# A stage of a two-layer pair kernel: the z product contracts 64 partitions instead of 128, and its padding and the clearing of it go

## The reference, cut to what matters

```python
g = sigmoid(xn @ Wg + bg)                    # xn: group norm of x; 128 -> 128 channels
z = einsum('bikc,bkjc->bijc', a, b)          # 16 channels
x1 = x + g * (layer_norm(z, g2, b2) @ Wz + bz)   # z: 16 -> 128 channels
```

## Time and profile before

| | us |
|---|---|
| median of 3 runs | 4713.67 |
| the profiled execution, its own time | 4714.6 |
| its span, first to last instruction | 4712.9 |
| PE busy with matmuls | 3987.0 |
| DVE busy | 3935.2 |
| ACT busy | 3377.8 |
| POOL busy | 2670.3 |
| first to last z product of stage 4 | 1165.5 to 1937.7 |

### The profile page before, as it was taken

One profiled execution on the slowest core, in us unless ns is written; L12 is line 12 of the kernel. 1 busy time (PEld: TensorE's weight loads), 2 busy tenths in 40 slices (PEclk: granted clock), 3 DMA queues, 4 the chain that ended last, 5 costly groups with the idle time before them and its releaser, 6 DMA issues. The chain is left out here.

```text
span 4712.9 us, 89415 instructions
## 1 busy us (share of the span) xinstructions
PE 3987.0 (85%) x26438; PEld 2239.9 (48%) x26438; DVE 3935.2 (83%) x5450; ACT 3377.8 (72%) x4840; POOL 2670.3 (57%) x1428
## 2 busy tenths in 40 slices
PE   0008999891999999799999999799999978888888
PEld 0005666441666666455555555355654434444444
DVE  5778888678888888899999999677789978777776
ACT  2337999553777777588888888566667768888887
POOL 0000000591888888588888888733334428888887
PEclk9999999995999999899999999899999989999999
DMA  9997999546999999799999999766678859999999
GB/s 366 410 405 261 364 369 366 176 134 202 392 391 390 390 390 391 268 311 319 321 322 321 320 320 322 271 230 223 231 254 305 305 186 406 407 403 405 403 402 354
DMA packets 700627, 1532.73 MB, mean 325 GB/s; under 512 B 32976, under 2 KB 50832, under 8 KB 698128
## 3 DMA queue, kind: packets, MB, share of 16 engines
q1 hardware_dynamic: 563696, 1263.31, 74.3%
q10 hardware_dynamic: 136864, 268.59, 14.9%
HBM read 1009.59 MB, written 522.19 MB: 325 GB/s over the span
## 5 line engine op out<-in xcount | busy, mean ns | idle before, releaser
L1766 POOL TENSOR_TENSOR s_oT<-s_gated,s7in_x1t 128x1024 f32<-128x1024 f32 x256 | 689.0, 2694 | 220.6 <-DVE s_gated L1685 215.4
L981 POOL TENSOR_TENSOR s_x1T<-s_gz,s_xT 128x512 f32<-128x512 f32 x512 | 652.1, 1274 | 127.9 <-DVE s_gz L947 123.2
L1432 PE MATMUL s_y_ps<-s_ab 128*128 128x512 f16 x3072 | 680.1, 380 | 2.0 <-DVE s_ab L1503 2.0
L1138 POOL TENSOR_TENSOR s_low<-s_xc,s_high 128x1024 f16<-128x1024 f32 x256 | 546.9, 2137 | 222.0 <-ACT s_high L1099 222.0
L878 PE MATMUL s_g_ps<-s_xT,s_Wg 128*128 128x512 f32 x1024 | 523.3, 593 | 0.0
L1685 DVE SCALAR_TENSOR_TENSOR s_gated<-s_p_ps,k_po_bias,s_gate 128x1024 f32<-128x1024 f32 x256 | 328.6, 1284 | 183.7 <-ACT s_gate L1722 164.0
L908 ACT ACTIVATE s_g<-s_g_ps,s_bg 128x512 f32<-128x512 f32 x512 | 351.7, 687 | 174.3 <-PE s_g_ps L878 174.3
L718 POOL MEMSET s_total<- 128x2048 f32 x1 | 1.8, 1809 | 837.9 <-POOLq L41 837.9
L1432 PEld LDWEIGHTS s_y_ps<-s_ab 128*128 128x128 f16 x3072 | 300.9, 98 | 344.8 <-issue 4.4
L947 DVE SCALAR_TENSOR_TENSOR s_gz<-s_z_ps,k_z_bias,s_g 128x512 f32<-128x512 f32 x512 | 384.4, 751 | 88.8 <-ACT s_g L908 86.5
L1104 ACT ACTIVATE s_gate<-s_g_ps,k_gi_bias 128x1024 f32<-128x1024 f32 x256 | 284.1, 1110 | 186.1 <-PE s_g_ps L1272 185.7
(11 more groups left out here) (225 smaller groups left out, 9499.8 us busy)
## 6 DMA issues: line engine op xcount, KB each, us to landing
s2in_xt<-in_x SPq DMA_DIRECT2D x128, 1024.0 KB, 9.6
s_xt<-in_x SPq DMA_DIRECT2D x256, 512.0 KB, 7.3
x_d<-s_x1T ACTq DMA_DIRECT2D x128, 1024.0 KB, 9.6
s5in_xt<-x_d SPq DMA_DIRECT2D x128, 1024.0 KB, 9.1
h_d<-s_h SPq DMA_DIRECT2D x128, 1024.0 KB, 6.8
s7in_x1t<-x_d SPq DMA_DIRECT2D x128, 1024.0 KB, 13.9
out<-s_ot ACTq DMA_DIRECT2D x128, 1024.0 KB, 9.3
s_mask_b<-mask_d SPq DMA_DIRECT2D x128, 512.0 KB, 4.8
```

The lines of the kernel that those rows point to most:

```text
L981: pool.tensor_tensor(x1T[:, i // U, i % U, :], gz[:, i % 4, :], xT[:, i % 8, :], ALU.add).then_inc(added, 1)
L1138: pool.tensor_tensor(low[:, n % 4, :, :], xc[:, n % 4, :, :], high[:, n % 4, :, :], ALU.subtract).then_inc(rest_ready, 1)
L1432: last = pe.matmul(y_ps[:, ib, 0:N], ab[:, u % 2, 0, a, kb, ib * P:(ib + 1) * P], ab[:, u % 2, 1, b, kb, :], start=m == 0, stop=m == len(t ...
L1766: pool.tensor_tensor(oT[:, n % 4, :, :], gated[:, n % 4, :, :], x1t[:, n // 2, 2 * (n % 2):2 * (n % 2) + 2, :], ALU.add).then_inc(added, 1)
```

## The change

`zt` has 64 partitions instead of 128, the z product names 64 partitions of the weights, and the clearing of the upper half, its semaphore and PE's wait for it are gone. All of it is in `stage4_layer0`. The loads, the order of the matmuls and all other waits stay. The weights' upper half is still cleared in the preparation (L204).

```diff
-        zt = s.sbuf("zt", [P, GROUPS, U, N], FP16)
+        zt = s.sbuf("zt", [64, GROUPS, U, N], FP16)
...
-        padded, folded, shifted, moments_ready, chain = s.sem("padded"), s.sem("folded"), ...
+        folded, shifted, moments_ready, chain = s.sem("folded"), ...
...
                 pe.wait_ge(folded, 2)
-                pe.wait_ge(padded, 1)
...
-                    pe.matmul(z_ps[:, i % 2, 0:N], K.Wz[:], zt[:, i // U, i % U, :], start=True, stop=True).then_inc(z_prod, 1)
+                    pe.matmul(z_ps[:, i % 2, 0:N], K.Wz[0:64, :], zt[:, i // U, i % U, :], start=True, stop=True).then_inc(z_prod, 1)
...
-                pool.memset(zt[64:128, :, :, :], 0.0).then_inc(padded, 1)
                 pool.sem_inc(added, 8)
```

More of the change, by code:

```diff
@@ L817, in stage4_layer0 @@
             s.sem(n) for n in ("turned", "kept", "g_prod", "z_prod", "sig", "mixed", "added", "counted")]
-        padded, folded, shifted, moments_ready, chain = s.sem("padded"), s.sem("folded"), s.sem("shifted"), s.sem("moments_ready"), s.sem("chain")
+        folded, shifted, moments_ready, chain = s.sem("folded"), s.sem("shifted"), s.sem("moments_ready"), s.sem("chain")
         @block_of(nc)
```

## The result

The changed kernel takes 4866.23 us, the median of 4 runs (4864.4 to 4867.33), against 4712.81 for the kernel before measured beside it: 1.0323 times as long, 95% interval 1.0306 to 1.0341. The profiled execution takes 4865.49 us, with a span of 4863.8.

What follows compares the result with a forecast made beforehand. PE's full list in stage 4 was taken as the bound: 0.096 + 0.098 + 0.105 = 0.299 us a step, 153 us over 512 steps, less 1.8 for the clear. Forecast median 4865 us, range 4810 to 4885.

Steps and rivals of the forecast that it cites:

- The bound: PE in stage 4, busy 100.00 of 100 us; any time added to its 1.51 us step counts 512 times.
- Into the smaller form: From the last transpose to the 64-row z product in stage 4, a change of form costs 0.096 us a step.
- Back: From the z product to the full-form gate product in stage 4, the change back costs 0.098 us a step.
- The exposed load: The gate product's weights, not loaded under the z product, add 0.105 us a step; bounds 0.011 and 0.161.
- The halved rows save nothing: The z product over 64 partitions still streams 512 columns and takes 0.215 us on PE, so nothing is gained.
- The clear: Without POOL's clear at stage 4's start, PE begins at 1160.2 instead of 1162.0, gaining 1.8 us once.
- Rival 1: PE fetches the gate's weights while it drains, leaving 0.20 us a step in stage 4: 4815 us; chance 0.15.
- rivals 2 and 3: Gate's exposed load 0.056 us as in a transpose, 4840 us, chance 0.06; or as at half clock, 4895 us, 0.08.
- Rival 4: Not slower: only joining two array halves costs, so stage 4's step stays 1.511 us: 4712 us; chance 0.06.
- Rival 5: The gaps in stage 4 drop PE to half clock, adding 770 us: 5640 us; chance 0.03.
- set nothing: In stage 4 the DMA share of 1.04 is no bound: no engine waits for a landing, transfers keep pace.

Runs made afterwards that it cites:

- the run with two rows to a step: Changed kernel with TensorE's step covering two rows: gate product, two 64-partition z products, gate product, eight transposes; 4794.26 us, 1.0175 times before.
- the kernel with the late clear: Kernel before, 128 partitions, with the clear moved behind VectorE's scaling and split in four parts, each awaited only when needed; 4711.72 us, 0.9996 of before.
- the run with four rows spread: Kernel with four rows' z products together as two pairs, gate products spread more evenly and VectorE's product one row further ahead; 4728.47 us, 1.0032 times before.

## Why the prediction was right

The forecast was 4865 us for the median, measured 4866.23. The mechanism is as forecast, term by term. That the sum comes within 1.2 us is in part luck: its terms are read from rows to 0.01 us, 5 us over 512 steps, and executions of one kernel differ by a few us.

*The bound.* TensorE's list filled the stage, so what is added to a step lengthens the stage by as much: 0.30 us a step, 153.2 us between the first and the last z product. The sum had 153.

*The terms.* Into the smaller form: 0.096 predicted, 0.20 - 0.11 = 0.09 measured, the same to the resolution of the rows. Back: 0.098 predicted, 0.32 - 0.215 = 0.10 measured. The exposed load: 0.105 predicted, 105 ns measured. This last term was the open one, with bounds of 0.011 and 0.161. It was found by adding to the excess of a transpose at full clock the difference of the two weight loads at full clock; the rule that the exposed part grows by what the load is longer, read at half clock, held at full clock. The order with transposes behind z shows the term by itself: the step is 0.047 us less, against 0.049. What the prediction didn't notice is that the rule holds for every matmul behind a change. A record is longer by the length of its weight load less 81 to 86 ns: the float32 product 105 at a load of 186 to 189, the float32 transpose 56 at 138 to 140, the fp16 product of stage 5 11 at 97, and the z product itself, 386 against 379, 7 at 92. Why it is this much, no run shows.

*The halved rows save nothing.* Right: two z products of 64 partitions on one half follow each other in 0.60 - 0.38 = 0.22 us in the run with two rows to a step, against 0.215 for the full product, and 32 partitions cost as 64.

*The clear.* PE's first transpose came 4.8 us after its last product instead of 6.5, 1.7 us earlier, where 1.8 was predicted, and it starts as the first load of x lands. That the gain reaches the end is not shown: with the clear kept the time is the same within its scatter.

*The rivals.* Rival 1 (weights hidden) fails by the 697 ns records, rivals 2 and 3 by their size. Rival 4 (only the joining of two halves costs) fails by the result, and by the run with 32 partitions, where no second part exists. Rival 5 fails by the granted clock of 1.00. Of the Trainium skill's two sentences, that of "TensorEngine Tiling (Array Packing)", "Key Properties", that a change of mode drains TensorE, agrees with what decided here, a gap of 0.09 to 0.10 us at each change of form; the traces show the gap and not what TensorE does in it. That of "TensorE: Matmul & The Clock Gate", "Why this matters for your kernels", that a single matmul over 32 partitions takes as long as one over 128, agrees with the product itself (a record of 385 ns in the run with 32 partitions, against 379 for 128) and says nothing of the step it stands in, which is 0.30 us longer.

*What the prediction said too firmly* is that the transfers "set nothing". They can at 1.511 us a row, but just: in the profiled execution of the kernel with the late clear, weight loads of the transposes waited 31.5 us in all for x, and the first to last z product took 1943.9 - 1164.1 = 779.8 us instead of 772.2. In the kernel before no such wait is seen. For a slower stage this did not matter; the run with four rows spread, which wanted a faster one, met it.

## What to carry to other kernels

Here a matmul over 64 or 32 rows was no cheaper than a full one, and between full ones it cost two changes of form of 0.1 us and the exposed load of the next weights: padding with zeros was the cheap choice, and 96 rows would have been as good. Narrow products lose less when they are gathered, so that changes of form are few, and laid on both halves, so that they run beside each other. By the terms, two pairs gathered should have gained; no arrangement tried here was faster than the padded kernel, since VectorE's waits and the transfers took over. To see this loss, look at the starts and at the number of matmuls in a window, not at PE's busy share.

## What the runs showed of the hardware

- Going from transposes (128 rows) to a product of 64 or 32 rows costs 0.09 to 0.10 us over the regular distance, back 0.10; 96 rows cost neither.
- Behind a change the first matmul is longer, by its weight load less 81 to 86 ns: 7 or 11 ns for fp16, 56 for a float32 transpose, 105 for a float32 product.
- A float32 scaling of 128 x 128 on VectorE takes 0.29 us, and 6.87 beside GpSimd's clear of 64 x 8192 fp16, which takes 6.92.
- Two products of 64 rows on the two halves of the array take the time of one: both lie in a record of 0.39 us, and the run is 55 us faster than with one half.
